# Fourier mixer on pairs of rows: block-diagonal transforms, both mixing weights of an axis held in SBUF, modes transposed straight from where they lie

## The reference, cut to what matters

```python
def _forward_fourier(x, fw0, fw1):
    xt = jnp.transpose(x, (0, 3, 1, 2))                     # b, i, m, n
    xfty = jnp.fft.rfft(xt, axis=-1, norm='ortho')
    wy = lax.complex(fw0[..., 0], fw0[..., 1])[..., :my]    # my = 25
    mixed_y = jnp.einsum('bixy,ioy->boxy', xfty[..., :my], wy)
    xy = jnp.fft.irfft(mixed_y, n=n, axis=-1, norm='ortho')
    xftx = jnp.fft.rfft(xt, axis=-2, norm='ortho')          # the same along the other axis
    mixed_x = jnp.einsum('bixy,iox->boxy', xftx[:, :, :mx, :], wx)
    xx = jnp.fft.irfft(mixed_x, n=m, axis=-2, norm='ortho')
    return jnp.transpose(xx + xy, (0, 2, 3, 1))
```

## Time and profile before

| | us |
|---|---|
| median of three runs | 10830.53 (10821.77 to 10856.01) |
| the profiled execution | 10839.46 |
| its span in the profile | 10837.6 |
| of this, the stretch of the changed stages, 7024 to 7523 | 499 |

### The profile page before, as it was taken

The page is one execution under the profiler, slowest core; times in us unless marked ns, Lnnn a source line. Parts: engine busy times, 40 slices in busy tenths (PEclk is TensorE's granted clock), DMA queues, the critical chain, the costliest instruction groups (busy, mean ns, idle before and its releaser), DMA issues. The chain is left out here.

```text
span 10837.6 us, 132369 instructions
## 1 busy us (share of the span) xinstructions
PE 8772.7 (81%) x41708; PEld 6246.0 (58%) x41708; DVE 7070.1 (65%) x9396; ACT 4526.0 (42%) x8541; POOL 4157.1 (38%) x2789
## 2 busy tenths in 40 slices
PE   5777777778777776799999999599748989896667
PEld 2444444444444443699999999588534444443445
DVE  6999899989988998444444444311256667653446
ACT  4666566656656665222222222122313444443231
POOL 3999599969977996111111111000000000000001
PEclk8999999999999998899999999766858999998678
DMA  4555355445544554000000000210310100003000
GB/s 130 165 161 164 111 162 163 144 129 161 162 131 144 160 163 128 16 14 12 14 10 14 14 12 10 76 35 21 125 37 22 24 18 14 21 11 126 16 25 18
DMA packets 332625, 835.00 MB, mean 77 GB/s; under 512 B 36307, under 2 KB 112247, under 8 KB 318301
## 3 DMA queue, kind: packets, MB, share of 16 engines
q1 hardware_dynamic: 331940, 826.57, 25.0%
HBM read 758.78 MB, written 39.08 MB: 74 GB/s over the span
## 5 line engine op out<-in xcount | busy, mean ns | idle before, releaser
L754 POOL TENSOR_TENSOR ss_work<-ss_dtu,ss_ringb 128x768 f32<-128x768 f32 x1536 | 2758.0, 1819 | 251.9 <-POOLq L59 248.5
L618 PE MATMUL ss_ps<-ss_work,ss_ident 128*128 128x512 f32 (+1 forms) x6144 | 2277.8, 517 | 446.4 <-POOL ss_work L764 327.4
L618 PEld LDWEIGHTS ss_ps<-ss_work,ss_ident 128*128 128x128 f32 x6144 | 1221.5, 203 | 1222.4 <-issue 877.7
L738 DVE TENSOR_TENSOR_SCAN ss_work<-ss_ps,ss_last,ss_work 128x768 f32<-128x768 f32 x1024 | 1811.4, 1802 | 96.0 <-issue 44.5
L671 ACT ACTIVATE ss_ps<-ss_dt,ss_a_neg 128x768 f32<-128x768 f32 x1536 | 1375.9, 896 | 273.1 <-DVE ss_work L738 254.6
L1234 ACT ACTIVATE stu_XT<-cv_ps 128x384 fp32r<-128x384 f32 x768 | 377.8, 492 | 1788.8 <-DVE cv_ps L1281 1361.4
L723 DVE TENSOR_TENSOR ss_work<-ss_work,ss_ps 128x1152 f32<-128x1152 f32 x768 | 1019.9, 1328 | 1.2 <-ACT ss_ps L679 1.2
L2233 ACT ACTIVATE at_probs<-at_ps 128x768 f32<-128x768 f32 x864 | 695.6, 811 | 705.6 <-PE at_ps L2187 705.0
L2251 DVE TENSOR_REDUCE at_top<-at_ps 128x1 f32<-128x384 f32 x1728 | 878.5, 553 | 164.7 <-PE at_ps L2171 163.1
L738 DVE TENSOR_TENSOR_SCAN ss_work<-ss_ps,ss_work 128x768 f32<-128x768 f32 x512 | 879.5, 1744 | 66.5 <-POOL ss_work L754 33.3
L1275 DVE TENSOR_TENSOR stu_XT<-cv_ps,stu_XT 128x384 fp32r<-128x384 f32 x768 | 428.4, 558 | 637.6 <-ACT stu_XT L1234 615.0
(11 more groups left out here) (546 smaller groups left out, 15466.7 us busy)
## 6 DMA issues: line engine op xcount, KB each, us to landing
ss_ringb<-scan_rows SPq DMA_DIRECT2D x768, 384.0 KB, 3.6
ss_ringc<-scan_rows SPq DMA_DIRECT2D x768, 384.0 KB, 3.7
c_w<-in_l_ffn_w SPq DMA_DIRECT2D x64, 1024.0 KB, 7.3
at_packs<-at_high SPq DMA_DIRECT2D x64, 288.0 KB, 5.5
cv_raw<-in_l_ffn_phi_odd SPq DMA_DIRECT2D x16, 576.5 KB, 3.7
cv_raw<-in_l_ffn_phi_even SPq DMA_DIRECT2D x16, 576.0 KB, 4.2
ffa_rows<-rows SPq DMA_DIRECT2D x16, 576.0 KB, 6.2
at_packs<-at_qk SPq DMA_DIRECT2D x32, 288.0 KB, 5.5
```

Of the source, the lines that this page charges most:

```text
L618: return pe.matmul(acc[:, d * WIN + a:d * WIN + e], ident[:, :], weighed[:, t % DEEP, d, a:e], start=n == 0 and e - a == 512, stop=n == NS ...
L738: dve.tensor_tensor_scan(hid[:, t % DEEP, d, ::step], decay[d][:, ::step], drive[:, t % DEEP, d, ::step], start, ALU.mult, ALU.add).then_i ...
L754: pool.tensor_tensor(drive[:, t % DEEP, d, :], dtu[:, t // NST % 2, d, :], ringb[:, t % RING, :], ALU.mult).then_inc(s["driven"], 1)
```

## The change

Two rows are handled as one operand of 96 partitions, and the transform matrices become block-diagonal (`np.kron(np.eye(2), ...)`): `dft` is 96x150 and `idft` 100x96.

- Stage a: 96 matmuls instead of 192 in an axis, each with 150 streamed columns; three fill a bank. The rows' buffer holds two images, so that four halves are in flight. In axis 0 a half is one DMA of 96 partitions, in axis 1 it is two DMAs of 48 partitions. The weights of all 25 modes of the axis are fetched in stage a too, by five DMAs of 640 KB into `ff_weights`, issued by SP behind the first two images and ahead of the last two.
- Stage b: the same 50 matmuls, with weights from `ff_weights`, and eight banks instead of five. Five semaphores for the weights are cleared behind it, with one more barrier.
- Stage c: the padded copy by ScalarE and the zeroing by GpSimd are gone. A transpose takes two rows of 50 modes (100 columns) straight from where VectorE wrote them, four of them to a group of eight rows: 96 transposes instead of 192 in an axis. One matmul for two rows: stationary 100 partitions by 128 columns, 96 columns streamed. The group after next is turned ahead of a group's matmuls, over four banks for either side.
- The loops are unrolled. Buffers are views of two tensors, `ff_early` (spectrum, then modes) and `ff_late` (rows, then mixed modes). The block that zeroed `idft` is gone.

```diff
 PAIRS = H // 2
-        rows = ctx.enter_context(nc.sbuf_tensor(name + "_rows", [W, H, C], F32))
+                def fetch(b):
+                        if b >= 2:
+                            sp.wait_ge(s["made"], 8 * (b - 2) + 4 + 4 * half)
...
+                fetch(0)
+                fetch(1)
+                for n in range(NF // NW):
+                    source = fw[n * NW * P:(n + 1) * NW * P, :].rearrange("(f c) x -> c f x", c=P)
+                    sp.dma_start(weights[:, n * NW:(n + 1) * NW, :, :].rearrange("c f m o -> c f (m o)"), source).then_inc(fetched.all[n], 16)
+                fetch(2)
+                fetch(3)
...
-                        for r in range(6):
-                            ins = pe.matmul(ps[:, n, r * 3 * NF:(r + 1) * 3 * NF], rows[:, 6 * n + r, :], dft[:, :], start=True, stop=True)
+                        for r in range(3):
+                            ins = pe.matmul(ps[:, n, r * 6 * NF:(r + 1) * 6 * NF], rows[:, b % 2, 3 * n + r, :], dft[:, :], start=True, stop=True)
...
-                pool.memset(stage[:, :, 2 * NF:], 0.0).then_inc(s["padded"], 1)
-                    act.activation(stage[:, :, 0:2 * NF], mixed[:, bass.ds(b * H, H), :], ACT.Copy).then_inc(s["staged"], 1)
+                def turn(g):
+                    if g >= 4:
+                        pe.wait_ge(s["kept"], g - 3)
+                    for r in range(4):
+                        pair = mixed[:, 8 * g + 2 * r:8 * g + 2 * r + 2, :].rearrange("c r k -> c (r k)")
+                        ins = pe.transpose(ps[0:4 * NF, g % 4, r * C:(r + 1) * C], pair, ident[:, :])
+                    ins.then_inc(s["turned"], 1)
+                def back(g):
+                    pe.wait_ge(s["kept"], g + 1)
+                    if g >= 4:
+                        pe.wait_ge(s["added"], g - 3)
+                    for r in range(4):
+                        ins = pe.matmul(ps[:, 4 + g % 4, r * 2 * W:(r + 1) * 2 * W], modes[:, g % 6, r, :], idft[:, :], start=True, stop=True)
+                    ins.then_inc(s["made"], 1)
+                turn(0)
+                turn(1)
+                for g in range(GROUPS):
+                    if g + 2 < GROUPS:
+                        turn(g + 2)
+                    back(g)
```

More of the change, by code:

```diff
@@ L1343, in fourier_mixer, with part @@
-        with nc.sbuf_tensor("ff_mx", [P, NR, 2 * NF], F32) as mixed:
-            for axis in range(2):
[L1345 to L1348, removed]
+        with ExitStack() as inner:
+            def part(name, shape):
+                return inner.enter_context(nc.sbuf_tensor("ff_" + name, shape, F32))
+            ident, dft, idft = part("ident", [P, P]), part("dft", [2 * W, 6 * NF]), part("idft", [4 * NF, 2 * W])
+            weights = part("weights", [P, NF, 2, C])
+            early, late = part("early", [P, 3 * NF * NR]), part("late", [P, 2 * PAIRS * 2 * C])
+            spectrum = early[:, :].rearrange("c (m f r) -> c m f r", m=3, f=NF)
+            modes = early[0:4 * NF, 0:6 * 4 * C].rearrange("m (u r c) -> m u r c", u=6, r=4)
+            rows = late[0:2 * W, 0:2 * PAIRS * C].rearrange("w (u q c) -> w u q c", u=2, q=PAIRS)
+            mixed = late[:, 0:NR * 2 * NF].rearrange("c (r k) -> c r k", r=NR)
+            load_all(nc, "ff_load", [(ident[:, :], w["ident"]), (dft[:, :], w["dft"]), (idft[:, :], w["idft"])])
+            for axis in range(2):
+                fetched = Signals(nc, f"ffw{axis}", " ".join(f"fetched{n}" for n in range(NF // NW)))
+                transform_rows(nc, f"ffa{axis}", axis, xn_dram, dft, rows, spectrum, w["fw"][axis], weights, fetched)
+                mix_modes(nc, f"ffb{axis}", weights, fetched, spectrum, mixed)
+                fetched.end()
+                inverse_rows(nc, f"ffc{axis}", axis, idft, ident, mixed, modes, HT)
@@ L1359, in transform_rows @@
         flat = spectrum[:, :, :, :].rearrange("c m f r -> c (m f) r")
+        PARTS = 1 + axis
         with nc.Block() as block:
@@ L1373, in _ @@
+                fetch(0)
[5 more added lines that the diff above has]
+                fetch(3)
             @block.tensor
             def _(pe):
-                with pe.Fori(0, B) as b:
+                for b in range(B):
@@ L1460, in _ @@
[L1460 to L1481 removed]
+                for g in range(GROUPS):
+                    act.wait_ge(s["turned"], g + 1)
+                    if g >= 6:
+                        act.wait_ge(s["made"], g - 5)
+                    act.activation(modes[:, g % 6, :, :], ps[0:4 * NF, g % 4, :].rearrange("m (r c) -> m r c", c=C), ACT.Copy).then_inc(s["kept"], 1)
```

144 lines of the change are left out of this document (50 added, 94 removed).

## The result

| | before | after |
|---|---|---|
| median, us | 10836.2 (10821.77 to 10856.01) | 10568.5 (10566.29 to 10572.27) |
| ratio, with its 95% interval | 1 | 0.9751 (0.9738 to 0.9765) |
| the profiled execution | 10839.46 | 10566.93 |
| its span | 10837.6 | 10565.1 |

The account below looks back on a forecast made before the run. TensorE's own stream was taken to set each stage's length. Gains of 81, 4 and 159 us sum to 244; 10839.5 less that is 10595.5, and 8.9 lower for the median gives 10,587 us, range 10,565 to 10,655.

Parts of the forecast that it names:

- The likeliest case: Whole kernel: stages a, b and c gain 81, 4 and 159 us, to 10,587 us; chance 0.62.
- Stage a, 100 us forecast: Stage a: 192 records an axis, bound by DMA or clock, 50 us per axis against 181 in all, minus 81.
- my 47 us: Stage a at full clock: DMA-bound, TensorE ends at 45.3 us, plus 1.7 for last copy and step.
- Stage b, 74 forecast: Stage b: no wait for first weights, one added barrier; 38.3 and 40 us become 2 x 37, minus 4.
- the bound of minus 10: Stage b: the larger gain, 10 us in place of 4, if the clock is up from the start.
- Stage c, 80 forecast: Stage c: 288 records an axis at 0.118 us, 40 us an axis against 239 in all, minus 159.
- the largest open term: TensorE's clock in stage c: taken as full, minus 159 us; at half clock minus 107.
- Rival 1: Clock stays at half in stage c, perhaps also a: 10,639 us, or 10,653 with stage a; chance 0.16.
- Rival 2: Stage a: weights load at 155 GB/s, not 349, each stage ends 12 us later: 10,611 us; chance 0.12.
- Rival 3: Unrolled stages: instruction fetches on TensorE's queue are not hidden, 0 to 21 us: 10,608 us; chance 0.07.

## Why the prediction held, and which of its terms were off

The likeliest case came: all three stages at or near full clock, no rival. The forecast was 10,587 and 10,568.5 came, 18.5 lower; counted within the changed stretch, 272.0 us against 244. That the total is nearer than the stages is luck in part: I took 8.9 us off because the profiled execution of before stood above its median, and after's profiled execution stands 1.6 below its own. The lengths of the stages after are compared below, and not the gains by stage, because the cuts above put the wait for the first weights into stage a of before and the padding into stage b.

- **Stage a, 100 us forecast for both axes, 87.9 measured.** Right were the spacing (0.127 and 0.248 us against 0.126 and 0.252), the start at half clock, the single wait for the fifth half and the second start at half clock behind it. Mis-sized was the load: I kept the 155 GB/s of the stretch in the earlier trace rows, "packets are as many and as small". After's halves came at 227 GB/s. The fifth half was there 27.8 us after the first issue (7052.05) instead of 30.9, and the wait was 6.66 us instead of 9. Behind it TensorE did not wait again (the last 96 records took 15.84 us, the restart included), so the loads did not bind the stage to its end, as my 47 us had it. Packets in axis 0 were indeed the same, and what held the 155 down came with the 48 partitions they went to: single rows with four halves in flight had 139 GB/s. The 9.4 us of the weights were right (346 GB/s against 349), though the row that I took the rate from, 6938 to 6948, is a store of the tokens and not their reload; the reload (6952 to 6965) ran at 346 too. Axis 1, where a half is two DMAs of 48 partitions each, side by side, ran at 241. The Trainium skill, "DMA: Bandwidth & Descriptors", Rules for kernel authors, says that two transfers to disjoint partition halves serialize and are not worth making. Had the pair run one behind the other, each at the 150 GB/s of halves that all go to the same 48 partitions, it would have stayed at 150; the trace, with 241, disagrees with "serialize" in this stretch. With the advice it agrees as far as it goes: one DMA of 96 partitions, in axis 0, had 227.
- **Stage b, 74 forecast, 69.4 measured.** The time per mode was right (32 us for 25 modes). The clock was up from the first matmul (1.00 in both axes, 0.93 and 0.90 before), which I had as the bound of minus 10. The added barrier was priced at 1.0 us: VectorE's last copy ends at 7102.85 and TensorE starts at 7104.14, 1.3 us for the whole step with that barrier in it. The step from a to b, which has none extra, is 0.96 us from the end of ScalarE's copy to TensorE. So it costs about 0.3.
- **Stage c, 80 forecast, 68.2 measured.** That nothing but TensorE sets its length held: 31.63 and 33.19 us busy of 33.3 and 34.8. Two terms were too dear. A record came every 0.110 us and not every 0.118 (288 of them: 2.4 us an axis), which was read from a stretch whose busy time held gaps. And the stage of axis 0 did not start at half clock, where I had put 3 us (in axis 1 the dip cost 1.6), nor did filling and draining take 3: it was 1.7.
- **The clock**, the largest open term, rose as I took it to. My reason for stage a, 96 partitions with a stream that never waits, held as a pair: with 48 partitions and the same stream the clock stayed at 0.50, and so it did with 96 partitions and 75 columns, where the stream waits for the loads. What fell is the later theory that the partitions alone bring it. Nor is a stream without waits needed everywhere: in stage c of after a record came every 0.110 us, where 96 columns would stream in 0.081 (at the 0.84 ns a column of stage b, an estimate), and the clock was full. Rival 1, which I priced at 0.16, may have been nearer than that, for stage c at 50 partitions falls to either side; with 100 none of the profiled stages stayed at half but those without look-ahead.
- **Transposes.** Stage c of axis 0 held 1.00 for 33 us, one record in three being a transpose. The Trainium skill, "TensorE: Matmul & The Clock Gate", Part 4 (PE-mode transpose), has it that the full rate does not engage for these; in a mixture with matmuls it did here, as in the stretch of transposes alone in the earlier trace rows.
- **Rival 2** (the loads set a longer stage) did not occur: the weights, with rows queued ahead of them and behind, moved at 346 GB/s (7038 to 7044), not at 155. Yet the queue's order did cost: 9 to 10 us an axis, which I had in the sum as a wait and did not see as something that another order would give back.
- **Rival 3 and unrolling.** The stretch has ten instruction packets on TensorE's queue, against nine by my count, and no TensorE wait that is put down to them; every idle time above 0.1 us is a DMA or the start of a stage:

```profile
q8 instruction: 10, 0.16, 0.3%
```

  What unrolling brings or costs by itself was not run.

## What to carry to other kernels

Before you count matmuls, look at the clock column of the stage: a TensorE that is busy 90% of the time at 0.50 has up to a factor of two in it, and wider operands (more partitions and more streamed columns, together) can fetch it, while either alone may not. A short wait costs more than its length where it takes the clock down, as the wait for the fifth half did (6.7 us, and 3.6 more TensorE time in the stage than without it); loads that nobody needs yet belong behind those that TensorE waits for. Undo each part of a bundle by itself: here the held weights were a loss in the place where they were queued.

## What the runs showed of the chip that I had not expected

- TensorE's clock can stay at 1.2 GHz in a stretch in which the engine's records leave no gap: 3.00 of 3.00 us busy with single rows (48 columns streamed on 50 partitions, transposes between), from 1.00 to 0.50 with no gap. Stage a stayed at 0.50 with 48 partitions and 150 columns, and with 96 and 75; with 96 and 150 it rose.
- The same stage took 40.3 us in one axis and 71.1 in the other, in one execution (50 partitions in stage c).
- Records that alternate between 128 and 50 partitions came 0.134 us apart at full clock; between 128 and 100, 0.110. The cause was not tried.
- Loads of rows ran at 139 and 150 GB/s into 48 partitions, with four of them queued, and at 227 and 241 into 96, by one DMA or by two side by side, both in pieces of 512 bytes (axis 0) and in long ones (axis 1). At 150 the DMA engines were busy for the whole time, so their busy share does not tell the one from the other.
